# Graph network kernel: TensorE drains behind each signalled group of products in the gather passes, and the drain raises the semaphore

## The reference

```python
# stage 0, three layers: mean over neighbours, then one dense layer
agg = segment_sum(x[src], dst); x = relu(concat([x, agg / (count + 1)]) @ W + b)
# stage 1: attention with 4 heads (softmax over the edges of each target), then a feed-forward net
alpha = exp(leaky_relu(a_src[src] + a_dst[dst]) - segment_max); out = segment_sum(xh[src] * alpha) / denom
# stage 2: messages with edge features, then two dense layers with batch norm
aggr = segment_sum(relu(h[src] + edge_attr), dst); z = (1 + eps) * h + aggr
# stage 3: plain sum of neighbours, and the edge features' sum
aggr = segment_sum(x[src] + edge_attr, dst)
```

## Time and profile before

| | |
|---|---|
| time, median of 3 runs | 14096.02 us (14094.08 to 14115.67) |
| the profiled execution's own time | 14089.3 us |
| its span | 14087.1 us |
| mean granted TensorE clock, share of full speed | 0.584 |
| gather passes: from the first gather's start to the last one's end | 304 to 2,364, 2,396 to 4,444, 4,473 to 6,690, 6,781 to 8,951, 9,505 to 11,673, 12,031 to 14,065 us |

### The profile page before, as it was taken

How to read it: one execution, slowest core, us unless ns; L and a number is a source line. 1 busy time by engine, 2 the same in 40 slices (tenths; PEclk the granted TensorE clock), 3 DMA queues, 4 the chain that set the end, 5 groups by cost and what they waited for, 6 DMA issues and landing times. The chain is left out here.

```text
span 14087.1 us, 101802 instructions
## 1 busy us (share of the span) xinstructions
PE 6019.7 (43%) x27042; PEld 4715.8 (33%) x27043; DVE 3432.9 (24%) x6131; ACT 1003.5 (7%) x1981; POOL 9588.9 (68%) x9490
## 2 busy tenths in 40 slices
PE   3444444333343444444344444664444446333333
PEld 2333333333333222232243433332222223333333
DVE  4222222111111222222344444351112224111111
ACT  1000000000000000000000000041111112000000
POOL 1777776777776666667577777307777771677777
PEclk9555555555555555555556556586676667555555
DMA  3222222222222222222233333223333332222222
GB/s 98 53 53 53 54 53 49 53 53 54 53 54 50 59 61 61 61 61 62 65 78 78 78 78 78 68 81 96 95 95 95 93 94 82 73 59 60 60 61 57
DMA packets 518282, 956.11 MB, mean 68 GB/s; under 512 B 173581, under 2 KB 327634, under 8 KB 516604
## 3 DMA queue, kind: packets, MB, share of 16 engines
q0 software_dynamic: 301056, 623.59, 17.9%
q1 hardware_dynamic: 217120, 331.46, 7.6%
HBM read 846.72 MB, written 107.67 MB: 68 GB/s over the span
## 5 line engine op out<-in xcount | busy, mean ns | idle before, releaser
L739 POOL DMA_INDIRECT work<-rows_a,index x4704 | 4644.8, 987 | 1742.5 <-issue 1533.1
L768 PE MATMUL psum<-onehot,work 128*128 128x80 f32 x12544 | 2634.4, 405 | 4251.7 <-DMA work<-rows_a,index 3045.6
L768 PEld LDWEIGHTS psum<-onehot,work 128*128 128x128 f32 x12544 | 2549.9, 314 | 4357.2 <-issue 4357.1
L1390 POOL DMA_INDIRECT regionC<-attention_rows,index x1568 | 1692.4, 1079 | 568.5 <-issue 477.6
L903 POOL DMA_INDIRECT work<-rows_b,index x1568 | 1666.3, 1063 | 582.5 <-issue 501.4
L739 POOL DMA_INDIRECT work<-rows_b,index x1568 | 1539.3, 982 | 541.4 <-issue 522.2
L975 PE MATMUL psum<-regionB,onehot 128*80 128x256 f32 x3136 | 910.8, 462 | 1235.5 <-ACT regionB L952 1235.5
L826 DVE TENSOR_TENSOR regionA<-regionA,psum 128x80 f32 x784 | 185.6, 237 | 4744.0 <-PE psum L768 4742.5
L975 PEld LDWEIGHTS psum<-regionB,onehot 128*80 128x80 f32 x3136 | 574.9, 187 | 1543.7 <-issue 1413.6
L182 POOL COPY work<-regionB 128x500 f32 (+1 forms) x75 | 45.2, 603 | 1040.6 <-DVE regionB L648 1040.6
L1036 DVE TENSOR_TENSOR regionB<-work,regionB 128x2048 f32<-128x2048 f32 x98 | 225.4, 2300 | 1727.8 <-DMA work<-rows_b,index 1727.8
(11 more groups left out here) (338 smaller groups left out, 6527.9 us busy)
## 6 DMA issues: line engine op xcount, KB each, us to landing
regionB<-in_edge_attr SPq DMA_DIRECT2D x195, 512.0 KB, 4.4
work<-rows_a,index POOLq DMA_INDIRECT x4704, 2.5
work<-rows_b,index POOLq DMA_INDIRECT x3136, 2.5
work<-edge_columns SPq DMA_DIRECT2D x98, 512.0 KB
regionC<-attention_rows,index POOLq DMA_INDIRECT x1568
x_transposed<-regionA SPq DMA_DIRECT2D x75, 250.0 KB, 6.1
rows_a<-regionC SPq DMA_DIRECT2D x50, 250.0 KB
h_transposed<-regionB SPq DMA_DIRECT2D x50, 250.0 KB, 2.4
```

What stands on the lines that cost most here:

```text
L739: pool.indirect_dma_start(rows3[h][:, t, :], None, table, bass.IndirectOffsetOnAxis(ap=net.index[:, k, h * ST + t:h * ST + t + 1], axis=0) ...
L768: last = nc.tensor.matmul(bank_of(h, q, 0), rows3[h][:, t, :], onehot[:, h * ST + t, :], start=(k == 0), stop=(k == GT - 1))
L1390: pool.indirect_dma_start(ring[s][:, t, :], None, net.XH, bass.IndirectOffsetOnAxis(ap=net.index[:, k, t:t + 1], axis=0)).then_inc(gathere ...
```

## The change

In each signalled group of the three functions the last product no longer raises the semaphore. Behind it TensorE executes a drain, an instruction that ends when the engine has finished what was issued, and the drain raises the semaphore. No product, load, wait or DMA is added, removed or put in another place, and the other engines' programs are the same. The dense chunks between the halves keep their semaphores on the products.

```diff
@@ aggregate, TensorE
                                 t = q * GT + k
-                                last = nc.tensor.matmul(bank_of(h, q, 0),
+                                nc.tensor.matmul(bank_of(h, q, 0),
                                                         rows3[h][:, t, :], onehot[:, h * ST + t, :],
                                                         start=(k == 0), stop=(k == GT - 1))
                             if extra:
-                                last = nc.tensor.matmul(bank_of(h, q, 1), net.ones[:, :],
+                                nc.tensor.matmul(bank_of(h, q, 1), net.ones[:, :],
                                                         piles[h][:, q * W:(q + 1) * W], start=True, stop=True)
-                            last.then_inc(summed[h], 1)
+                            pe.drain().then_inc(summed[h], 1)
@@ edge_pass, TensorE
-                        m.then_inc(packed[h], 1)
+                        pe.drain().then_inc(packed[h], 1)
...
-                        t.then_inc(turned[h], 1)
+                        pe.drain().then_inc(turned[h], 1)
@@ gat_pass, TensorE: sums_of, lift, turn
-                    m.then_inc(packed[h], 1)
+                    pe.drain().then_inc(packed[h], 1)
...
-                    t.then_inc(summed[h], 1)
+                    pe.drain().then_inc(summed[h], 1)
...
-                    T.transpose(score_t, score_of[k], net.ident[:, :]).then_inc(score_ready, 1)
+                    T.transpose(score_t, score_of[k], net.ident[:, :])
+                    pe.drain().then_inc(score_ready, 1)
...
-                    t.then_inc(windows, 1)
+                    pe.drain().then_inc(windows, 1)
...
```

More of the change, by code:

```diff
@@ L981, in turn @@
                         for x in range(2 * GPH):
-                            t = T.transpose(bank(2 + h)[:, x * W:(x + 1) * W], staged[h][:, x * D:(x + 1) * D],
+                            T.transpose(bank(2 + h)[:, x * W:(x + 1) * W], staged[h][:, x * D:(x + 1) * D],
                                             net.ident[0:W, 0:W])
-                        t.then_inc(turned[h], 1)
+                        pe.drain().then_inc(turned[h], 1)
                 each(pe, r, turn)
@@ L1491, in sums_of @@
                             t = h * HALF + q * GT4 + i
[L1492 removed]
+                            T.matmul(bank(6 + h)[q % 2 * W4:(q % 2 + 1) * W4, q // 2 * XW:(q // 2 + 1) * XW],
                                          onehot[k][:, t, :], ring[s][:, t, :],
                                          start=(i == 0), stop=(i == GT4 - 1))
[L1495 removed]
+                    pe.drain().then_inc(packed[h], 1)
                 def lift(n, h):
@@ L1501, in lift @@
                         T.transpose(bank(5)[:, x * P:(x + 1) * P], held[x][:, 0:D], net.ident[:, :])
-                        t = T.matmul(bank(5)[32:32 + 2 * H, 256 + x * P:256 + (x + 1) * P], held[x][:, D:XW],
+                        T.matmul(bank(5)[32:32 + 2 * H, 256 + x * P:256 + (x + 1) * P], held[x][:, D:XW],
                                      net.ident[:, :], start=True, stop=True)
-                    t.then_inc(summed[h], 1)
+                    pe.drain().then_inc(summed[h], 1)
                 def turn(j, n, s, k, f3, f2):
@@ L1514, in turn @@
                     for g in range(2 * GQ):
-                        t = T.transpose(bank(1)[:, g * 2 * H:(g + 1) * 2 * H], cuts[:, g * P:(g + 1) * P],
+                        T.transpose(bank(1)[:, g * 2 * H:(g + 1) * 2 * H], cuts[:, g * P:(g + 1) * P],
                                         net.ident[64:64 + 2 * H, 64:64 + 2 * H])
-                    t.then_inc(windows, 1)
+                    pe.drain().then_inc(windows, 1)
                     if not first:
@@ L1525, in turn @@
                     T.matmul(bank(1)[0:H, 129:130], net.ident[64:64 + 2 * H, 64 + H:64 + 2 * H], cuts[:, 0:1],
-                             start=True, stop=True).then_inc(chained, 1)
+                             start=True, stop=True)
+                    pe.drain().then_inc(chained, 1)
                     if not first:
@@ L1531, in turn @@
                     for q in range(HALF):
-                        m = T.matmul(bank(4)[:, q * 16:(q + 1) * 16], flipped[:, q * P:(q + 1) * P],
+                        T.matmul(bank(4)[:, q * 16:(q + 1) * 16], flipped[:, q * P:(q + 1) * P],
                                      blocks[:, q // 2 * 16:q // 2 * 16 + 16], start=True, stop=True)
-                    m.then_inc(own_ready, 1)
+                    pe.drain().then_inc(own_ready, 1)
                     pe.wait_ge(carried_ready, n + 1)
-                    T.matmul(bank(1)[:, 192:256], sel_t, carried, start=True, stop=True).then_inc(spread, 1)
+                    T.matmul(bank(1)[:, 192:256], sel_t, carried, start=True, stop=True)
+                    pe.drain().then_inc(spread, 1)
                     pe.wait_ge(max_ready, n + 1)
-                    T.transpose(max_e, back, net.ident[:, :]).then_inc(max_turned, 1)
+                    T.transpose(max_e, back, net.ident[:, :])
+                    pe.drain().then_inc(max_turned, 1)
                     pe.wait_ge(alpha_ready, n + 1)
                     T.matmul(bank(1)[:, 256:257], head_select(net), alpha, start=True, stop=True)
-                    T.matmul(bank(1)[:, 257:258], den_select, alpha, start=True, stop=True).then_inc(alpha_spread, 1)
+                    T.matmul(bank(1)[:, 257:258], den_select, alpha, start=True, stop=True)
+                    pe.drain().then_inc(alpha_spread, 1)
                     if not first:
```

2 lines of the change are left out of this document (1 added, 1 removed).

## The result

The changed kernel takes 14150.11 us (median of 11 runs, 14135.86 to 14159.34), the kernel before 14104.07 us on the same chip (11 runs, 14093.55 to 14126.05). The ratio is 1.0031, with a 95% interval of 1.0023 to 1.0039. The profiled execution of the changed kernel took 14147.38 us with a span of 14145.2 us, at a mean granted clock of 0.581.

What follows compares the result with a forecast made beforehand. Pool's own issue was taken to bound five of six passes, a closed loop through TensorE's sums the third aggregation pass. Loop 26, ends 6 and collisions 8 us made 40 on 14096: 14136 us, 8-in-10 range 14095 to 14180.

Steps and rivals of the forecast that it cites:

- The closed loop: Third aggregation pass: both halves' sums are in a chain Pool waits for; 1.08 us, 24 times, 26 us (12 to 41).
- The two breaks: Third pass loop: the next group starts later behind a drain, 0.52 us in half 1 and 0.46 in half 0.
- The sum of 0.52: Break between a half's groups on TensorE, including 0.20 us restart and 0.07 slower first product; bounds 0.2 to 0.8.
- The signal: Each signalled group: the drain ends, and so raises the semaphore, 0.05 us behind the last product's recorded end.
- The sequencer's cover: Third pass: TensorE's reading of due chunks' numbers behind the drain costs nothing, with 1 us of cover.
- The other passes: Outside the third aggregation pass, drains hide: 0.6 us against 11.8 us of room in an aggregation half.
- The ends of the passes: Drains where nobody gathers any more: 2.4 us aggregations, about 0.3 edge pass, 3 attention pass; together 6 us.
- The collisions: DVE's compares move by 0.6 us in Pool's cycle, pulling passes towards their mean: +8 us, bounds -40 and +50.
- The cheap drain: Rival, chance 0.18: TensorE restarts in the drain's shadow, break 0.2 us, collisions cancel; 14111 us.
- the hidden one: Rival, chance 0.08: no closed loop, or the drain ends before the product's signal would have come; 14096 us.
- The cover of the sequencer: Rival, chance 0.11: chunk-number reads pass their cover by 1 us, 24 us more, or collisions turn out dear; 14160 to 14190.
- A faster kernel: Rival, chance 0.05: compares in all 392 halves get cheaper, from 0.74 us to 0.59; about 14065 us.

Runs made afterwards that it cites:

- product signals: Against the kernel before: last products raise the semaphore, a drain without one follows, in all four aggregation passes only; 14141.26 us, ratio 1.0040.
- two drains: Against the kernel before: two drains behind each group of the third aggregation pass only, the second raising the semaphore; run twice, ratios 1.0053 and 1.0034.
- later compare: Against the kernel before: no drains, VectorE reads one number before each compare in the first and last aggregation pass; two runs, ratios 0.9993 and 1.0002.

## Why the prediction was right, and where its terms were off

**The sum.** 40 us were forecast, 46 measured, with an interval of 32 to 55 by the ratio. The predicted 14136 lies 14 us under the measured median; 8 of these are in the base, since the kernel before took 14104 in this comparison.

**The closed loop held.** The stalls of the 24 loops grew by 29.3 us (172.4 to 201.7, labels with their gaps) where 26 were forecast, the pass by 30.2 in this execution and 28.0 and 28.6 in the two others with drains in it. Averaged over the 24 loops of kernel before, after, and product signals, read from single records (us):

| part of the loop | before | after | product signals | forecast |
|---|---|---|---|---|
| half 1, first product to last one's end | 6.97 | 7.47 | 7.46 | +0.52 |
| its end to L1263 | 2.97 | 2.99 | 2.98 | +0.05 |
| L1263 to L1277 | 30.90 | 31.21 | 30.94 | 0 |
| L1277 to half 0 | 1.40 | 1.45 | 1.45 | 0 |
| half 0, first product to last one's end | 3.81 | 4.24 | 4.23 | +0.46 |
| its end to Pool's gather | 0.81 | 0.83 | 0.81 | +0.05 |
| sum with the landing of half 1's rows | 48.80 | 50.24 | 49.90 | |

The two breaks came out at 0.50 and 0.43 us against 0.52 and 0.46. The hole between starts is 0.22 + 0.42 = 0.64 us, forecast 0.7, and half 1 takes 7.61 us in its median, forecast 7.6. The row of the attention pass that served as the price of a restart (0.22 us) was the right neighbour: the idle time between groups is 0.22 us too, so the 0.05 for the drain's end and the 0.20 for the restart were one and the same 0.22, and the slower first products made up the rest (in half 1 0.50 us behind the idle time, 0.42 within the group). The four terms of the forecast together measure 0.97 us a loop, 23 us, against 1.08 and 26. The loop grew by more, 1.44 us after and 1.10 with the product's signals: the rest is the chunk, told below, the step from L1277 to half 0 (0.05 us) and 0.1 us in the landing, which the last row holds too (1.94, 2.05 and 2.04 us), and which has no term in the forecast. Pool's wait took up 1.2 us of it.

The sum of 0.52 holds 0.20 for the last product's end, for which the prediction gives no row, and neither does it for the 0.46; no run shows either term by itself. What the traces show in their place: in the kernel before the 32 records of half 1 take 7.12 us, 0.22 each, and a record lasts 0.42, so the last one ends 0.20 us behind where the next would have started. Behind a chunk, at a granted clock of 1.00, the 64 records of both halves take 7.37 us, 0.115 each, and the shortest record lasts 0.27, so there it is 0.16.

**The signal** was late by 0.02 us, not 0.05. That is 24 x 2 x 0.02 = 1 us, and the experiment with the product's signals confirms that it doesn't matter. The 0.05 was read from a drain that the kernel has the earlier trace rows, and all four of line 721 end 0.05 us behind the last product's recorded end, in the kernel before and in the one after; the 1,519 added ones end 0.02 us behind it. The runs put the cost on the drain's standing between groups (28 to 30 us in the third pass with either way of signalling), not on who raises the semaphore.

**Not foreseen: the chunk.** L1263 to L1277 grew by 0.31 us in the kernel after and by 0.27 in the one with drains in the third pass only, but by 0.04 with the product's signals. The first product of line 1268 was at the long duration (1.20 us, the short one is 0.69) in 12 of the 24 chunks before, 18 after, 17 and 12 in these two, and 14 and 11 in the executions without drains in this pass. The granted clock tells the two kinds apart. Two stretches of the kernel after, at this product in the first chunk and in the second (us, busy us of each engine, clock, DMA):

```profile
4582.80:4584.00 1.20, 1.20 (x2) 0.50 (x2) 0.00 (x0) 0.00 (x0) 0.90 (x2) 0.50 0.34 101
4676.50:4678.00 1.50, 1.10 (x2) 0.30 (x2) 0.30 (x2) 0.00 (x0) 1.19 (x2) 1.00 0.47 150
```

In some chunks the clock is granted at 1.00 for 3.4 us around this product, from 1.0 to 2.3 us ahead of it, and falls back to 0.50; in the others it stays at 0.50 until the chunk's end. A chunk of the first kind takes 30.1 to 30.5 us from L1263 to L1277, one of the second 31.4 to 31.5. The 6 chunks that changed kind are thus 6 of the 7 us that L1263 to L1277 grew by in this pass. The kernel with the product's signals has the same breaks and half of its chunks of each kind, as before; whether the drains push the others or it only differs from execution to execution is left open.

**The sequencer's cover** held. DVE's own pause is still 1.67 us, and TensorE starts L1263 2.97 us after its wait began, where it was 2.95: it waits for DVE, and had read the numbers by then. In the median of the 24 chunks these reads end 2.4 us ahead of the end of half 1's last product in the kernel before, and 1.73 us behind it in the one after, 1.24 us ahead of L1263.

**The other passes** hide their drains, as forecast: L739 in the last pass is never released late, L903 not at all. In the attention pass the new label "PEq L1495" has 3.7 us in 12 plain gaps of 0.3 us at most.

**The ends of the passes** were put at 6 us. Between the passes, the gaps of before and after differ by 0.6, -0.4, 0.1, -5.1 and 5.1 us, and the tail by 0.6. The sum is 1 us, and what the two large ones hide can't be told from their scatter (the gap ahead of the last pass moved by 7.4 in the kernel with drains in the other aggregations, which has none in the edge pass before it). The term was likely too large.

**The collisions** were the term with the least ground. The last pass was to lose 13 us; it lost 12.9, 13.7 and 9.1 in the three executions with drains in it, and 3.3 and -2.1 in those without. Pool's means in that pass are 986, 987 and 984 ns with drains, and 978, 979 and 977 without: no overlap. What the gathers take beyond the undisturbed ones of their own execution is 63.0, 68.1 and 63.4 us there with drains and 53.9, 51.8 and 52.0 without, so 9 to 16 us are collisions. Most of that (8 to 12 us) is in gathers that overlap a compare.

The rule behind it is in the earlier trace rows and was not read there: the gather that starts at 1005.52 ends at 1007.68, 0.82 us behind the compare's end (1006.86), and the one that starts at 1029.20 ends at 1030.77, 0.81 us behind 1029.96. In the four aggregation passes of the six executions at 14.1 ms, the gather that follows a compare's start and overlaps it ends 0.82 us behind the compare's end in 9 of 10 cases (0.812 to 0.821), wherever it started. So a compare costs Pool about 0.12 us plus the time that has gone by since the last gather's start: 0.17 us right behind that start, 0.57 at 0.4 to 0.5 us, 0.96 at 0.8 to 0.9 and 1.27 at 1.1 to 1.2, and it falls back to 0.15 as the next gather begins (medians). A compare that starts early in the cycle and is moved by half a microsecond gets dearer by just that much. In the last pass 49, 53 and 54 of the 98 compares start within 0.25 us of a gather's start without drains, and 32, 30 and 22 with them.

The rule by which I got there, each pass drawn to the mean of the four, fails in the rest: the second pass was to lose and shows 982, 978 and 977 ns with drains against 982, 981 and 979 without, the first was to win and shows 999, 994 and 995 against 994, 998 and 997. The attention pass gained 4.9 us after and 8.4 in the kernel with drains there and in the edge pass; of the 4.9, 3.6 are the slower undisturbed gathers of that execution. Over all six passes the collisions are 666 us before and 673 after, +6 where +8 was forecast, and 654 to 676 in the other four executions, so the sum is within their scatter. That it came out near is luck; the last pass's part is not.

**What the sum is made of.** The kept executions of before and after differ by 58 us in their spans. 29 are the third pass's waits, 22 the undisturbed gathers (2.3 ns more for each of 9,408), 6 the collisions and 1 the ends. The 22 don't belong to the change: undisturbed gathers take 945.8 to 945.9 ns in this execution, in the one with drains in the third pass only, in one of the two with two drains and in one that has no drain at all (the kernel in which Pool waits for each group, second batch), and 943.4 to 943.5 in the other ten, whatever drains they have. That leaves 36 us with a cause, 29 of them forecast at 26. The median says 46, with an interval that reaches down to 32; what the other 10 are, if they are anything, is open.

**The rivals.** The cheap drain (14111) fell with the stalls' +29 us, the hidden one as well. The cover of the sequencer did not go. A faster kernel would have needed compares cheaper than in any pass; with 6 us more over all passes they got no cheaper.

## What to carry to other kernels

- A drain between two groups that would otherwise follow each other without a break costs 0.4 to 0.5 us on TensorE here. It is kernel time only where TensorE's work is in a closed loop: 1,519 drains cost 46 us, and 48 of those in the middle of a half, two for each chunk, make 24 x (0.50 + 0.43) = 22 of them.
- Look for that loop in the waits first. A pass with 24 waits of 7 us among 63 labels tells where TensorE counts; the page's shares (Pool 68%) say that it never does.
- A shift of half a microsecond in another engine's stream can move an engine that waits for nothing, by its collisions (9 to 16 us in the last pass here). Which way can't be had from the passes' means, but from where the one starts in the other's cycle: here a gather caught by a compare ends 0.82 us behind the compare, so its price grows with the compare's distance from the last gather's start.
- Compare the undisturbed instructions of two executions before you put a difference down to the edit: 2.3 ns a gather was 22 us here, and it came with drains and without.

## What the runs showed of the hardware beyond this

The same kernel took 14,092 us in one batch and 15,408 and 15,431 us in the later ones, at nearly the same granted clock (0.584, 0.572 and 0.573). In the later batches the gathers of Pool take what they take in the first (0.94 us and 0.30 us of gap), and their rows land as early (the last packet 1.24 us behind the gather's end in the last pass, median, against 1.26), but TensorE's signals come late. The timeline of the last pass in the kernel with the later compare, second run:

```profile
13508.09 7.11 PE L768 MATMUL psum<-onehot,work 128*128 128x80 f32 x32 [20.65 <-DMA work<-rows_a,index]
13515.93 0.24 DVE L829 TENSOR_TENSOR regionA<-regionA,psum 128x80 f32 x1 [24.02 <-PE psum L768]
13528.18 7.11 PE L768 MATMUL psum<-onehot,work 128*128 128x80 f32 x32 [12.98 <-DMA work<-rows_a,index]
13530.69 0.24 DVE L829 TENSOR_TENSOR regionA<-regionA,psum 128x80 f32 x1 [14.52 <-remote]
```

Half 0's sums end by the records at 13515.20, but DVE adds the second group at 13530.69, 15.5 us later and 2.5 us after half 1's sums have begun; in the kernel before of the first traces it is 0.22 us in every half. In this pass the median delay of half 0's two groups is 5.3 and 15.5 us, that of half 1's 1.7 and 0.22 us. Pool, which waits for the same semaphore, then loses 2 to 6 us in each of some 48 iterations. The drains agree: with two drains (third batch), the first one of a half 0 ends in its median 2.3 us behind the last recorded product, and 10 us at most, while in the kernel after all 196 of the third pass end 0.02 us behind it. The record of the semaphores agrees too: it has updates of half 0's at 13515.70 and 13530.48, while its groups end at 13511.79 and 13515.20. The traces of the later batches hold only 63,000 to 68,000 updates of semaphores where the first six hold some 174,600, which is why many waits there are put down to "remote" or "issue".

In these traces drains and waiting engines go on later than the product's record ends: the first drain of a half 0 by 2.3 us in the median with two drains, DVE's add of half 0's second group by 15.5 us with the later compare. Why that is so there, and for half 0 above all, is not known from these runs; neither is whether it belongs to a chip.
